# 64-wide products of a blockwise triangular inverse in 32-wide halves, with other owners for its block copies and a few scales and sums moved

## The chip, the cores and the metric

The kernel runs on one core of a Trainium2 chip. A core has five engines that run their own instruction streams and meet through semaphores: PE (TensorE, matrix products and transposes into PSUM), DVE (VectorE), ACT (ScalarE), POOL (GpSimd) and SP (SyncE, which here only issues DMA). The metric is the device time of one launch in microseconds (us); lower is better.

## The reference

The input x has 4 sequences of 1024 tokens with 128 channels. Everything is f32. Cut to what matters:

```python
def _layernorm(x, axis=-1, eps=1e-05):
    ...
    return (x - m) / jnp.sqrt(v + eps)

def delta(x, gates_w, gates_b, lr_w, lr_b, out_w, out_b):
    qkv = x @ gates_w + gates_b
    q, k, v = jnp.split(qkv, 3, axis=-1)
    lr = x @ lr_w + lr_b
    k = k / jnp.linalg.norm(k, axis=-1, keepdims=True)
    K = jnp.tril(jnp.einsum('ntc,nsc->nts', k, k), k=-1)
    A = K + jnp.eye(T, dtype=x.dtype)
    u = jax.scipy.linalg.solve_triangular(A, v, lower=True)
    score = jnp.einsum('nsk,ntk->nst', q, k)
    y = jnp.einsum('nst,ntv->nsv', score, lr * u)
    return y @ out_w + out_b
...
h = _layernorm(x)
h = h + delta(layernorm(h, dn_g, dn_b), ...)
h = h + mlp(layernorm(h, mn_g, mn_b), w1, b1, w2, b2)
x = x + h
h = _layernorm(x)
# top-1 of 8 experts by h @ gate_w.T, each a 128x128 matrix
x = x + h + expert_out_of_the_chosen_expert(h)
```

## The kernel before

Tokens are cut into T = 8 tiles of 128 tokens. A tile holds the same 128 tokens of all NS = 4 sequences, so most steps of a tile are four products of 128x128, or one instruction over 512 columns. `LOW` means sequences 0 and 1, `HIGH` 2 and 3. The tiles form two groups g of TG = 4.

**Front.** For each tile DVE takes the statistics (`stats`), ACT a square root (`root`), DVE the reciprocal (`scales`), and POOL, ACT and DVE share the normalised rows `xh`. PE turns them (`xT_`), ACT copies them out (`xnT_`), PE projects them to k (`kT_`), ACT copies that, and PE multiplies k by its own transpose (`gram`) into a 128x128 matrix per sequence, which ACT copies to `gg_all`. `k_` turns k back.

**Inverse of the unit triangular matrix.** Its 128 rows are four blocks b of 32. The diagonal 32x32 blocks of a whole group (16 matrices, four blocks each, 128 partitions) are gathered into `gd`: 26 small DMAs on SP in all, ten of them for group 0, and three copies on ACT and three on DVE. `prepare(0)` on DVE waits for all of these. DVE then inverts all blocks of the group at once: `prepare`, the 31 steps of `eliminate`, and two transposes into `d_all` (the inverse, `plain_`) and `dT_all` (its transpose, `turned`). The blocks must then stand at their places in `tt_all` (the 128x128 transposed inverse of a tile) and `da_all` (inverses as a left operand). For the group's first tile DVE (`place`) and ACT (`plain_place`, `turned_place`) copy them, for the other three tiles six DMAs on SP do.

**Joining.** For each tile, blocks are joined to 64 and then to 128: `ya` (eight products of 32x32), `za` (twelve), `y64_` (four of 64x64), `t12` (four of 64x64), each followed by a copy out of PSUM under the same name on ACT, and for `yb`, `zb` and `t12` on ACT in group 0 and on DVE in group 1.

**Recurrence.** The state S runs over the tiles: `ks` (k times state, PE), `rv_` (DVE, the right-hand side), `w_` (inverse times it, PE; ACT copies), `lrw` (ACT, times the learning rate), `s_` (PE, adds to the state; ACT copies it out as `sm`). The joins of tile t+1 stand between these. While group 1 is being eliminated on DVE, tiles 1 to 3 of the recurrence run, and `rv_all(1)`, `rv_all(2)` and `rv_all(3)` stand between the steps of `eliminate(1)` and behind it.

**The rest.** After the last tile the state is folded with the weights (`mm`, `mw`, `gn`), and each tile goes through h (normalised x, `h_` on DVE for HIGH, POOL for LOW) plus delta (`h2_`), statistics, scale and bias (`hscale`, `hbias`), MLP, again statistics, and the experts, with `copy_predicated` on DVE. POOL makes the sums `xb2_` (x plus a bias) and `xb_` (plus h) into `x_all`.

All orders are written out by hand; every engine executes its own list in that order. Nothing is scheduled by a planner.

## Time and profile before

| | us |
|---|---|
| median of three runs | 202.74 (202.15 to 202.99) |
| the profiled execution, its own time | 201.71 |
| its span | 199.8 |
| PE busy | 179.8 (90%) |
| DVE busy | 166.3 (83%) |
| ACT busy | 114.4 (57%) |
| POOL busy | 63.7 (32%) |

The span is what the profiler sees between the first and the last instruction; the execution's own time lies 1.9 us above it. The parts follow one another in time: the front to about 23 us for group 0 (35 us for group 1), values and preparations to 51, the recurrence to 98, the fold and the first tile of the rest to 112, the steady loop of the rest to 186, its tail to the end. Times of a row are counted from the span's start.

### The profile page before, as it was taken

The numbers are of one execution on the slowest core, as the hardware profiler recorded it, in microseconds if no ns is written. First come the engines' busy times: TensorE is split into PE (matmuls) and PEld (weight loads), VectorE is DVE, ScalarE is ACT, GpSimd is POOL, SyncE is SP. The second block draws the span as 40 slices with busy tenths as digits, with TensorE's granted clock in tenths as the row PEclk, the third lists the DMA queues.
The fourth block names the chain that finished last, engine by engine and source line by source line (L and its number), as shares of the span: only waits on it lengthen the run. The fifth ranks groups of instructions, "written<-read, shape, count | busy, mean of one in ns | idle before, by whom it ended". The sixth has DMA issues, their size and how long they took to land.

```text
span 199.8 us, 4189 instructions
## 1 busy us (share of the span) xinstructions
PE 179.8 (90%) x1299; PEld 130.7 (65%) x1299; DVE 166.3 (83%) x750; ACT 114.4 (57%) x318; POOL 63.7 (32%) x79
## 2 busy tenths in 40 slices
PE   0498799999999899999998999999999999999980
PEld 0355676887988677877864776766667675657540
DVE  7898899999899945494686688898989899878885
ACT  2567786588795785457327763645456363752420
POOL 8256980000000069980022220070605233202030
PEclk9999999999999999999999999999999999999997
DMA  4982011103000030000000000010101001011011
GB/s 115 302 211 29 10 16 20 21 5 59 3 2 3 0 61 1 3 3 3 0 2 0 3 0 0 0 54 3 53 0 36 18 5 53 0 53 53 0 54 53
DMA packets 20265, 6.53 MB, mean 33 GB/s; under 512 B 9995, under 2 KB 20244, under 8 KB 20244
## 3 DMA queue, kind: packets, MB, share of 16 engines
q1 hardware_dynamic: 19668, 6.21, 13.1%
q8 instruction: 10, 0.16, 0.4%
q10 hardware_dynamic: 576, 0.07, 0.2%
q14 instruction: 11, 0.09, 0.1%
HBM read 3.15 MB, written 2.10 MB: 26 GB/s over the span
## 4 chain that ended last, share of the span: by engine, by line
PE 62%; DVE 17%; ACT 5%; issue 3%; DVEq 0%; ACTq 0%
PE ps L1390 25%; PE ps L1104 10%; PE ps L1298 5%; PE ps L1099 5%; PE ps L1369 4%; DVE kT_all L1022 3%; DVE xi L836 3%; DVE prod L829 3%; PE ps L1133 2%; PE ps L1288 2%; DVE rv L885 2%; PE ps L1226 2%; PE ps L1282 2%; PE ps L1213 2%; PE ps L1116 1%
## 5 line engine op out<-in xcount | busy, mean ns | idle before, releaser
L1390 PE MATMUL ps<-ewC,kT_all 128*128 128x256 f32 (+2 forms) x192 | 62.0, 455 | 0.7 <-DVE kT_all L1022 0.7
L1022 DVE COPY_PREDICATED kT_all<-mask,ps 128x256 f32<-128x256 int32 x112 | 49.1, 439 | 2.6 <-DVE mask L1008 0.3
L1390 PEld LDWEIGHTS ps<-ewC,kT_all 128*128 128x128 f32 x192 | 33.9, 190 | 16.6 <-issue 6.0
L359 POOL TENSOR_TENSOR x_all<-x_all,kT_all 128x512 f32<-128x512 f32 (+1 forms) x8 | 9.6, 1204 | 54.6 <-ACT kT_all L679 54.6
L836 DVE TENSOR_TENSOR xi<-xi,prod 128x60 f32<-128x60 f32 (+13 forms) x116 | 19.6, 207 | 0.3
L829 DVE TENSOR_TENSOR prod<-lts,xi 128x60 f32<-128x60 f32 (+13 forms) x116 | 19.3, 204 | 0.3
L353 POOL TENSOR_TENSOR x_all<-x_all,h_all 128x512 f32<-128x512 f32 (+1 forms) x9 | 10.3, 1150 | 24.6 <-DVE h_all L954 19.9
L1298 PE MATMUL ps<-ww,k_all 128*128 128x256 f32 (+1 forms) x72 | 17.1, 365 | 0.4 <-DVE ww L939 0.4
L322 POOL TENSOR_SCALAR h_all<-x_all,mv,rr 128x128 f32<-128x128 f32 x18 | 14.6, 822 | 7.5 <-DVE rr L751 7.5
L649 ACT ACTIVATE k_all<-h_all,nb,rr 128x128 f32<-128x128 f32 x32 | 13.4, 483 | 1.9 <-DVE nb L975 1.5
L336 POOL TENSOR_SCALAR bob<-bob 128x128 f32<-128x128 f32 x1 | 0.5, 528 | 42.5 <-DVE da_all L859 42.5
L340 POOL TENSOR_SCALAR h_all<-x_all,mv,rr 128x128 f32<-128x128 f32 x16 | 12.5, 795 | 0.0
L1099 PE MATMUL ps<-ident,h_all 128*128 128x128 f32 x32 | 5.8, 312 | 7.3 <-ACT h_all L390 7.2
L1298 PEld LDWEIGHTS ps<-ww,k_all 128*128 128x128 f32 x72 | 11.1, 189 | 2.0 <-DVE ww L939 0.5
L1099 PEld LDWEIGHTS ps<-ident,h_all 128*128 128x128 f32 x32 | 4.4, 160 | 12.1 <-issue 12.0
L638 ACT ACTIVATE sd<-mv,epsc 128x4 f32<-128x4 f32 (+1 forms) x9 | 2.6, 294 | 15.0 <-DVE mv L966 15.0
L655 ACT ACTIVATE k_all<-ps,cols 128x512 f32<-128x512 f32 (+1 forms) x9 | 6.6, 730 | 8.1 <-PE ps L1099 8.1
L1104 PE MATMUL ps<-kT_all 128*128 128x128 f32 x64 | 9.5, 292 | 1.9 <-ACT kT_all L399 1.8
L679 ACT ACTIVATE kT_all<-kT_all,rr 128x128 f32<-128x128 f32 x30 | 9.5, 388 | 2.3 <-DVE kT_all L1022 2.3
L559 ACT ACTIVATE ww<-ww,v_all 128x128 f32<-128x128 f32 x28 | 10.7, 407 | 0.1
L666 ACT COPY kT_all<-ps 128x512 f32<-128x512 f32 (+1 forms) x9 | 4.8, 535 | 10.0 <-PE ps L1099 10.0
L1104 PEld LDWEIGHTS ps<-kT_all 128*128 128x128 f32 x64 | 8.0, 196 | 3.7 <-ACT kT_all L399 3.4
(156 smaller groups left out, 389.9 us busy)
## 6 DMA issues: line engine op xcount, KB each, us to landing
x_all<-in_L_attn_x_dram SPq DMA_DIRECT2D x7, 256.0 KB, 5.4
out_dram<-x_all SPq DMA_DIRECT2D x7, 256.0 KB, 2.3
ew<-in_L_ffn_expert_w_dram SPq DMA_DIRECT2D x1, 512.0 KB
gd<-gg_all SPq DMA_DIRECT2D x26, 16.0 KB, 1.8
tt_all<-dT_all SPq DMA_DIRECT2D x8, 48.0 KB, 2.1
x_all<-in_L_attn_x_dram SPq DMA_DIRECT2D x2, 128.0 KB, 2.8
out_dram<-x_all SPq DMA_DIRECT2D x2, 128.0 KB, 1.8
da_all<-d_all SPq DMA_DIRECT2D x4, 48.0 KB, 2.1
```

The lines of the kernel that those rows point to most:

```text
L322: nc.gpsimd.tensor_scalar(xh[:, t, n], x_all[:, t, n], mv[:, 0, t, n, 0:1], rr[:, t, 1, n:n + 1], ALU.subtract, ALU.mult).then_inc(xh_pool, 1)
L340: last = nc.gpsimd.tensor_scalar(h_all[:, t, n], x_all[:, t, n], mv[:, 0, t, n, 0:1], rr[:, t, 0, n:n + 1], ALU.subtract, ALU.mult)
L353: nc.gpsimd.tensor_tensor(x_all[:, t, span(of)], x_all[:, t, span(of)], h_all[:, t, span(of)], ALU.add).then_inc(xb_ready, len(of))
L559: nc.scalar.mul(ww[t % 2][:, n, C:2 * C], ww[t % 2][:, n, 0:C], v_all[:, t, n, C:VW]).then_inc(lrw_ready, 1)
L649: nc.scalar.activation(tn[t % 2][:, n], h_all[:, t, n], ACT.Identity, bias=nb2[:, t, n:n + 1], scale=rr2[:, 0, t, n:n + 1]).then_inc(tn_re ...
L829: nc.vector.tensor_tensor(mul[half], lts[:, j, lo:hi].unsqueeze(2).broadcast_to([P, hi - lo, w]), xi[g][:, j, 0:w].unsqueeze(1).broadcast_ ...
L836: nc.vector.tensor_tensor(xi[g][:, lo:hi, 0:w], xi[g][:, lo:hi, 0:w], mul[half], ALU.subtract).then_inc(elim, 1)
L1022: nc.vector.copy_predicated(sel[t % 2][:, n], mask[t % 2][:, n, E - 1 - e].unsqueeze(2).broadcast_to([P, 2, F]), expert(e)).then_inc(picke ...
L1099: last = nc.tensor.transpose(tiles(bank)[:, n], src(n), ident[:])
L1104: last = nc.tensor.matmul(tiles(bank)[:, n], lhsT(n), rhs(n), start=True, stop=True)
L1298: last = nc.tensor.matmul(both(n)[:, of], k_all[:, t, n], ww[t % 2][:, n, of], start=t == 0 and n % 2 == 0 and of.start == 0, stop=True, s ...
L1390: last = nc.tensor.matmul(dst, x1T[t % 2][:, 2 * pair + n], ewC[:, of], start=True, stop=True)
```

## The change

- `y64_` and `t12` on PE multiply with 32 moving columns instead of 64: each 64x64 product becomes two of 64x32. The halves of `y64_` go to PSUM partitions 0 to 63 and 64 to 127, so that ACT copies [128 x 128] instead of [64 x 256]; the halves of `t12` read partitions 0 to 63 and 64 to 127, and write to banks 6 and 7. For this `da_all` has all 128 partitions, with its blocks there twice: `za` has one more product per sequence and its copy one more instruction on ACT, and two more DMAs per group. `ya` now also waits for the copy of the tile before's `t12`.
- Placing for the first tile of a group: DVE's `place` is gone; ACT places three blocks (`plain_place`, `odd_place`), SP's DMAs the rest, of all four tiles. SP issues eight DMAs a group instead of six, in another order, the ones for `t12` ahead of those for the next tile's `ya`.
- Front: for the first three tiles `gram` and its copy stand one tile later; `k_` stands one tile earlier from there on.
- Scales: `root` and `scales` only treat the scale of the doubly normalised rows; that of h is made once for all tiles, by one add and one reciprocal on DVE and one square root on ACT, while tile 4 is joined. `nb` is only made where ACT reads it. POOL's `h_` therefore waits for `first_rr`.
- DVE: 12 and 11 elimination steps instead of 10 and 12 between the `rv_all` of group 1, and `rv_all(3)` ahead of the two transposes. At tile 4, `ya`, `za`, `y64_` and `t12` stand later on PE, and DVE's `rv` on both sides of `zb`. `h_` of the last two tiles stands behind the last `ww`.
- POOL's first `xb_` wait for the first tile's `hbias` (`hnb_done`).

Front, PE, from the first projection on (`xnT_all,gall` is `kT_`, `ident,h_all` is `xT_`, `kT_all` alone is `gram`, `ident,kT_all` is `k_`). Before:

```order
L1116 MATMUL ps<-xnT_all,gall 128x512
L1099 MATMUL ps<-ident,h_all 128x128 x4
L1104 MATMUL ps<-kT_all 128x128 x4
L1116 MATMUL ps<-xnT_all,gall 128x512
L1099 MATMUL ps<-ident,h_all 128x128 x4
L1104 MATMUL ps<-kT_all 128x128 x4
```

Now:

```order
L1144 MATMUL ps<-xnT_all,gall 128x512
L1127 MATMUL ps<-ident,h_all 128x128 x4
L1144 MATMUL ps<-xnT_all,gall 128x512
L1127 MATMUL ps<-ident,h_all 128x128 x4
L1132 MATMUL ps<-kT_all 128x128 x4
L1144 MATMUL ps<-xnT_all,gall 128x512
L1127 MATMUL ps<-ident,h_all 128x128 x4
L1132 MATMUL ps<-kT_all 128x128 x8
```

The first `gram` stands behind the second tile's `kT_` and the third's `xT_`; the second and third follow each other.

DVE, from the end of the second elimination to the first reciprocal for POOL (`rv<-v_all,nk,ps` is `rv_`; `d_all`, `dT_all` the two transposes; `yT` is `yb`; a `tt_all<-ps` of 32 is `zb`, of 64 `t12`). Before:

```order
L844 STREAM_TRANSPOSE d_all<-xi 128x32x16
L849 STREAM_TRANSPOSE dT_all<-d_all 128x512
L885 SCALAR_TENSOR_TENSOR rv<-v_all,nk,ps 128x128 x4
L858 COPY tt_all<-dT_all 32x4x32 x2
L859 COPY da_all<-d_all 32x4x32
L867 COPY yT<-ps 32x128
L863 STREAM_TRANSPOSE nk<-nkl 128x32
L872 TENSOR_SCALAR tt_all<-ps 32x4x32
L885 SCALAR_TENSOR_TENSOR rv<-v_all,nk,ps 128x128 x4
L878 TENSOR_SCALAR tt_all<-ps 64x4x64
```

Now:

```order
L906 SCALAR_TENSOR_TENSOR rv<-v_all,nk,ps 128x128 x4
L874 STREAM_TRANSPOSE d_all<-xi 128x32x16
L879 STREAM_TRANSPOSE dT_all<-d_all 128x512
L884 STREAM_TRANSPOSE nk<-nkl 128x32
L888 COPY yT<-ps 32x128
L939 TENSOR_SCALAR ab<-mv 128x8x4
L906 SCALAR_TENSOR_TENSOR rv<-v_all,nk,ps 128x128 x2
L893 TENSOR_SCALAR tt_all<-ps 32x4x32
L906 SCALAR_TENSOR_TENSOR rv<-v_all,nk,ps 128x128 x2
L899 TENSOR_SCALAR tt_all<-ps 64x2x4x32
L948 RECIPROCAL rr<-sd 128x8x4
```

The `rv` of tile 3 is ahead of the transposes, the placing copies are gone, and the reciprocal that POOL waits for stands behind `t12` of tile 4.

PE at the same place (`rv,tt_all` is `w_`, `ww,k_all` is `s_`, `sm,kT_all` is `ks`, `tt_all,gg_all` of 32 is `ya`; `yT` and `da_all` rows are `za`), before (the `za` rows that repeat are left out):

```order
L1288 MATMUL ps<-rv,tt_all 128x128 x4
L1181 MATMUL ps<-tt_all,gg_all 32x32 x8
L1298 MATMUL ps<-ww,k_all 128x256 x2
L1195 MATMUL ps<-yT,d_all 32x32
...
L1298 MATMUL ps<-ww,k_all 128x256 x2
L1213 MATMUL ps<-tt_all,gg_all 64x64 x4
L1282 MATMUL ps<-sm,kT_all 128x128 x4
L1226 MATMUL ps<-y,da_all 64x64 x4
L1181 MATMUL ps<-tt_all,gg_all 32x32 x8
L1288 MATMUL ps<-rv,tt_all 128x128 x4
```

Now:

```order
L1322 MATMUL ps<-rv,tt_all 128x128 x4
L1332 MATMUL ps<-ww,k_all 128x256 x4
L1210 MATMUL ps<-tt_all,gg_all 32x32 x8
L1316 MATMUL ps<-sm,kT_all 128x128 x2
L1224 MATMUL ps<-yT,d_all 32x32
...
L1316 MATMUL ps<-sm,kT_all 128x128 x2
L1242 MATMUL ps<-tt_all,gg_all 64x32 x8
L1254 MATMUL ps<-y,da_all 64x32 x8
L1210 MATMUL ps<-tt_all,gg_all 32x32 x8
L1322 MATMUL ps<-rv,tt_all 128x128 x4
```

All four joins of tile 4 now stand behind the state update of tile 3.

The diff, cut to its core:

```diff
@@ the blocks of one tile on SP @@
             sp.wait_ge(tt_clear, 2)
+            sp.wait_ge(da_clear, 1)
             for g in range(NG):
+                def turned(b, lo):
+                    r = slice(Q * b, Q * b + Q)
+                    return by_block(tt_all, g, r, b, lo), dT_all[g][r, lo * NS:GN]
+
+                def plain(b, at, lo):
+                    r, place = slice(Q * b, Q * b + Q), slice(Q * at, Q * at + Q)
+                    return by_block(da_all, g, place, b, lo), d_all[g][r, lo * NS:GN]
+
+                sp.wait_ge(d_done, g + 1)
+                dst, src = plain(1, 1, 0)
+                sp.dma_start(dst, src).then_inc(rest_sent[g], 16)
                 sp.wait_ge(dT_done, g + 1)
...
-                for (dst, src), sent in ((turned(1), odd_sent), (turned(3), odd_sent), (plain(0), even_sent),
-                                         (turned(2), even_sent), (plain(1), rest_sent), (turned(0), rest_sent)):
+                for (dst, src), sent in ((turned(2, 0), two_sent), (turned(0, 0), rest_sent), (plain(0, 2, 0), rest_sent),
+                                         (plain(1, 3, 0), rest_sent), (turned(1, 1), odd_sent), (turned(3, 1), odd_sent),
+                                         (plain(0, 0, 1), zero_sent)):
                     sp.dma_start(dst, src).then_inc(sent[g], 16)
@@ POOL @@
-            pool.wait_ge(tt_dve, NG)
+            pool.wait_ge(dT_done, NG)
...
             pool.wait_ge(xT_mm, T)
+            pool.wait_ge(first_rr, 1)
...
+            pool.wait_ge(hnb_done, 2)
             xb_(0, LOW)
+            pool.wait_ge(hnb_done, NS)
             xb_(0, HIGH)
@@ ACT: the front, the copies of za and y64, tile 4 @@
-            for t in range(T):
+            for t in range(TG):
                 if t == TG - 2:
                     root(4)
                 kT_(t)
                 if t == TG - 1:
                     root(5)
-                if t + 1 < T:
-                    xnT_(t + 1)
+                xnT_(t + 1)
                 if t == 0:
                     root(3)
                 if t + 2 < TG:
                     xh_(t + 2)
-
-                if t >= TG:
-                    k_(t - TG)
+                if 0 < t < TG - 1:
+                    gg_(t - 1)
+                if t == TG - 2:
+                    gd_(t)
+                    gg_(t)
+            gd_(TG - 1)
+            k_(0)
...
-                nc.scalar.mul(da_all[Q:2 * Q, t, :, 0:Q],
-                              ps[Q:2 * Q, 6, 2 * NS * Q:3 * NS * Q].rearrange("p (n c) -> p n c", n=NS), -1.0).then_inc(za_ready, 1)
+                for b in (1, 3):
+                    r = slice(Q * b, Q * b + Q)
+                    last = nc.scalar.mul(da_all[r, t, :, 0:Q],
+                                         ps[r, 6, 2 * NS * Q:3 * NS * Q].rearrange("p (n c) -> p n c", n=NS), -1.0)
+                last.then_inc(za_ready, 1)
...
                 if t == TG - 1:
+
+                    s_(t, 0)
+                    odd_place(1)
                     s_(t, 1)
+                    plain_place(1)
+                    ya(t + 1)
+                    za(t + 1)
                     y64_(t + 1)
+                    act.wait_ge(first_ab, 1)
+                    nc.scalar.activation(sd[:, :, 0], ab[:, :, 0], ACT.Sqrt).then_inc(first_sd, 1)
@@ DVE @@
-            place(0)
 
             prepare(1)
-            eliminate(1, 0, 10)
+            eliminate(1, 0, 12)
             dve.wait_ge(nk_done, 1)
             dve.wait_ge(v_ready, T)
             rv_all(1)
-            eliminate(1, 10, 22)
+            eliminate(1, 12, 23)
             rv_all(2)
-            eliminate(1, 22, Q - 1)
+            eliminate(1, 23, Q - 1)
+            rv_all(3)
             plain_(1)
             turned(1)
-            rv_all(3)
-            place(1)
...
+            h_(T - 2)
+            h_(T - 1)
             dve.wait_ge(mw_mm, 2)
@@ PE: the joins @@
                 for n in range(NS):
-                    last = nc.tensor.matmul(ps[0:2 * Q, 7, 2 * n * Q:2 * (n + 1) * Q], gg_all[2 * Q:4 * Q, t, n, 0:2 * Q],
-                                            tt_all[2 * Q:4 * Q, t, n, 2 * Q:4 * Q], start=True, stop=True)
+                    for h in range(2):
+                        last = nc.tensor.matmul(ps[2 * Q * h:2 * Q * h + 2 * Q, 7, n * Q:n * Q + Q], gg_all[2 * Q:4 * Q, t, n, 0:2 * Q],
+                                                tt_all[2 * Q:4 * Q, t, n, (2 + h) * Q:(3 + h) * Q], start=True, stop=True)
                 last.then_inc(y64_mm, 1)
...
                 for n in range(NS):
-                    last = nc.tensor.matmul(ps[0:2 * Q, 7, 2 * (NS + n) * Q:2 * (NS + n + 1) * Q], da_all[:, t, n],
-                                            y64[t % 2][:, n], start=True, stop=True)
+                    for h in range(2):
+                        r = slice(2 * Q * h, 2 * Q * h + 2 * Q)
+                        last = nc.tensor.matmul(ps[0:2 * Q, 6 + h, (3 * NS + n) * Q:(3 * NS + n + 1) * Q], da_all[r, t, n],
+                                                y64[t % 2][r, n], start=True, stop=True)
```

## Rows read from the trace of the kernel before

**Rows 1.** The page: the span, and the shares of the chain that ended last.
```profile
span 199.8 us, 4189 instructions
PE 62%; DVE 17%; ACT 5%; issue 3%; DVEq 0%; ACTq 0%
```

**Rows 2.** That chain in order: start us, length us, what.
```profile
77.33 1.13 PE ps L1288 x8
```

**Rows 3.** Timeline, front: start us, us, engine, line, out<-in, count, idle before.
```profile
12.49 3.12 POOL L322 TENSOR_SCALAR h_all<-x_all,mv,rr 128x128 f32<-128x128 f32 x4 [2.14 <-DVE rr L751]
...
13.54 0.58 ACT L415 COPY gg_all<-ps 128x512 f32<-128x512 f32 x1 [0.20 <-PE ps L1104]
...
23.35 1.96 DVE L802 STREAM_TRANSPOSE lt<-gd 128x1024 f32<-128x1024 f32 x1
```

**Rows 4.** SP's DMAs issued between 17 and 19.5 us; landings of that line.
```profile
17.04 2.53 SPq L270 DMA_DIRECT2D gd<-gg_all  x4
...
DMA to landing us min/median/max: 1.8/1.8/2.9
```

**Rows 5.** Timeline of DVE, from the first inverse's transpose to the second group.
```profile
44.11 0.71 DVE L849 STREAM_TRANSPOSE dT_all<-d_all 128x512 f32<-128x512 f32 x1
...
45.64 1.95 DVE L802 STREAM_TRANSPOSE lt<-gd 128x1024 f32<-128x1024 f32 x1
```

**Rows 6.** Timeline during the second elimination: DVE, and PE's weights of one ks.
```profile
55.17 1.12 DVE L885 SCALAR_TENSOR_TENSOR rv<-v_all,nk,ps 128x128 f32<-128x128 f32 x4 [0.97 <-PE ps L1282]
...
62.65 1.11 DVE L885 SCALAR_TENSOR_TENSOR rv<-v_all,nk,ps 128x128 f32<-128x128 f32 x4
...
68.05 0.97 PEld L1282 LDWEIGHTS ps<-sm,kT_all 128*128 128x128 f32 x8
...
69.65 1.08 DVE L885 SCALAR_TENSOR_TENSOR rv<-v_all,nk,ps 128x128 f32<-128x128 f32 x4
```

**Rows 7.** Timeline of PE and ACT, one tile of group 1: joins and copies.
```profile
79.83 0.68 PE L1213 MATMUL ps<-tt_all,gg_all 64*64 64x64 f32 x8
80.44 1.13 PE L1298 MATMUL ps<-ww,k_all 128*128 128x256 f32 x4
...
83.19 0.44 PE L1181 MATMUL ps<-tt_all,gg_all 32*32 32x32 f32 x16
...
79.97 0.27 ACT L496 ACTIVATE da_all<-ps 32x128 f32<-32x128 f32 x1
```

**Rows 8.** Weight loads, each: ns min/median/max, first and last start us, form.
```profile
L1213 PEld LDWEIGHTS ps<-tt_all,gg_all x64: 129/135/136, 47.9 to 92.7; 64*64 64x64 f32 x64
...
L1159 PEld LDWEIGHTS ps<-gwT,cent x2: 186/188/189, 42.2 to 42.3; 128*128 128x128 f32 x2
```

**Rows 9.** Timeline of PE at 42 us: loads of 128 columns for 8 moving ones.
```profile
42.19 0.30 PEld L1159 LDWEIGHTS ps<-gwT,cent 128*128 128x128 f32 x2 [0.44 <-ACT ewT L465]
```

**Rows 10.** Timeline of DVE, then of POOL: the scales and sums of h.
```profile
79.19 1.33 DVE L890 TENSOR_SCALAR h_all<-x_all,mv,rr 128x128 f32<-128x128 f32 x4
...
85.44 3.39 DVE L890 TENSOR_SCALAR h_all<-x_all,mv,rr 128x128 f32<-128x128 f32 x4
...
72.05 12.50 POOL L340 TENSOR_SCALAR h_all<-x_all,mv,rr 128x128 f32<-128x128 f32 x16
84.52 2.48 POOL L347 TENSOR_TENSOR x_all<-x_all,b2s 128x512 f32<-128x512 f32 x2
```

**Rows 11.** Timeline of DVE at the last tile of the recurrence.
```profile
94.72 0.42 DVE L878 TENSOR_SCALAR tt_all<-ps 64x256 f32<-64x256 f32 x1 [1.91 <-PE ps L1226]
...
96.18 1.11 DVE L890 TENSOR_SCALAR h_all<-x_all,mv,rr 128x128 f32<-128x128 f32 x4
```

**Rows 12.** Timeline of DVE, biases of the first and second tile, and POOL beside.
```profile
105.31 1.23 DVE L975 SCALAR_TENSOR_TENSOR nb<-mv,rr 128x2 f32<-128x2 f32 x1
...
109.96 0.16 DVE L975 SCALAR_TENSOR_TENSOR nb<-mv,rr 128x4 f32<-128x4 f32 x1
...
105.26 1.27 POOL L353 TENSOR_TENSOR x_all<-x_all,h_all 128x512 f32<-128x512 f32 x1 [1.45 <-DVE h_all L954]
```

182 lines of the change are left out of this document (93 added, 89 removed).

## The prediction

> **What bounds the kernel now.** I read the page first: PE holds 62% and DVE 17% of the chain that ended last [rows 1]. That is an average; read in order of time, the chain changes engines four times, and the edits lie only in the first 110 us. Up to 23.35 us the front ends with the gathering of `gd`, on which DVE's first elimination waits [rows 3]. From there to about 70 us DVE works almost without a gap; its one gap inside the second elimination is 0.97 us ahead of `rv_all(1)` [rows 6]. From the `w_` of tile 4, at 77.33 us [rows 2], to 98 us PE is full. From 98 to 110 us the first tile's chain of small steps decides, and behind it comes the loop that the change leaves alone. So I follow four times: the start of the first elimination, the three `rv_all`, the `w_` of tiles 4 and 7, and the second bias.
>
> **Front.** Three things make the old path shorter: each stage of the statistics and each `nb` loses a short instruction, and `gram` no longer holds up PE. By my count of the chain DVE could transpose `gd` at about 22.0. But the first copy to `gg_all` started at 13.54 and now stands behind the turned rows of tile 2. POOL makes two of these from 12.49, 0.78 us each, so until 14.05 [rows 3], now some 0.5 sooner for the instructions left out (taken, not measured; with 0 it all comes 0.5 later); then `xT_` (about 0.7), `gram` (about 1.1), and ACT's copies ahead put `gg_all` at 15.5 to 16.1. It was done at 14.1, so the first gathering DMA goes out 2.0 us later. SP issues four in 2.53 us, 0.63 to 0.65 each, and each lands 1.8 us after its issue [rows 4]. Group 0 needs ten: 16.1 + 9 x 0.65 + 1.8 = 23.75. In the kernel before the first went out at about 14.3, but SP idled ahead of tiles 1 and 2, and the tenth landed at about 22.5, hidden behind DVE. Now the DMAs are the last to end: **+0.4 us** instead of -1.3. The bounds: -0.3 if `gg_all` starts 0.7 sooner, +1.3 if the second `kT_` still runs at the slow pace of the first (one us longer), because PE has less to do ahead of it.
>
> **The first inverse to `rv_all(1)`.** `place` goes from DVE: the turned inverse is done at 44.82 and the next group's transpose begins at 45.64 [rows 5], so 0.8 us of DVE are free. The joins of tiles 0 and 1, however, hang on PE and ACT: `rv_all(1)` came at 55.17, 10.35 us behind the turned inverse. ACT's three placing copies cost what DVE's did; the fifth DMA of the eight, the last that `t12` needs, is issued 0.1 + 3 x 0.65 us behind the turned inverse and lands 2.1 later, at +4.2, against +4.9 when `t12` ran. `za` costs ACT one copy of 0.27 us more per tile [rows 7], the copy of `y64_` perhaps 0.1 less. I keep 10.35: `rv_all(1)` at 55.17 + 0.4 = 55.6. DVE's elimination stood idle for 0.97 us there; now it does two steps more, of (62.65 - 56.25) / 12 = 0.53 us each [rows 6], and is ready at 54.9. So it is 1.07 - 0.4 = 0.65 us ahead in work. **`rv_all(2)`**: 55.6 + 1.05 + 11 x 0.53 = 62.5, with one step more done. **`rv_all(3)`** no longer waits for the transposes but for `ks` of tile 3. Its weights loaded at 68.05, 5.4 us behind `rv_all(2)` [rows 6]; that gives 68.35, where it was 69.65: **-1.3 us**. DVE waits there (eight steps end at 67.3), and the inverse ends at 68.35 + 1.1 + 1.85 = 71.3, not 69.7.
>
> **Tile 4.** Here the gain is used up. Before, `ya` and `za` of tile 4 ran between the products of tile 3. Now `w_` of tile 3 starts at 68.7, its `s_` ends 3.5 later at 72.2 (1.3 until ACT has copied and scaled the first two, then two halves of 1.13 at best [rows 7]), ACT copies the state and places a block (0.3 to 0.4 each), and only then, at 72.9, comes `ya`. From there in one chain: `ya` 0.44, copy 0.28, `za` 0.4, copy 0.28, `y64_` 0.68, copy 0.27, `t12` 0.68 and its copy 0.42 [rows 7, 11], with some 0.07 between each two: 76.9. `ya` of tile 5 now waits for that copy and stands ahead of `w_`: 77.3. It was 77.33 [rows 2]. Net **0**, with bounds of -0.6 and +0.6.
>
> **Halves of the joins.** The trace has no 64x32 product. A 64-wide product takes 0.68 us for eight instructions [rows 7]; a product of 8 moving columns with 128 weight columns has its two loads 0.11 us apart [rows 9], so below the load's own time fewer moving columns buy nothing. A load takes 53 ns more at 128 columns than at 64 [rows 8], so 64 columns need about 55 ns, near what an instruction takes today. The 32-wide `ya` does two products to different parts of the array in 33 ns (16 in 0.44 [rows 7]), so halves do run side by side. Eight pairs of 55 ns: **0**. Lower bound 33 ns a pair, -0.2 us a product; upper bound all sixteen in a row, +0.45.
>
> **POOL's scales later.** POOL started them at 72.05, and they took 12.50, then its sums came; now it starts at 77.4, so the sums lie from 89.9 to 95. DVE's four `h_` take 1.33 beside POOL's scales and 3.39 beside its sums [rows 10]. The slow ones move from tile 6's joins, where PE had other work, to those of tile 7, which have no `ya` behind them: `h_` from 91.7 to 95.1 lets the copy of `t12`, at 94.72 [rows 11], start at 95.15: **+0.45 us**. Then the last `h_` no longer stand between `rv` and `ww`: 1.11 us [rows 11], of which 0.2 turns into waiting for `w_`: **-0.9**. Their new place, ahead of a copy that waits over a us, costs nothing as long as POOL's sums are over by 97.
>
> The rows show no blocking beside POOL's scales. The Trainium skill (SBUF — State Buffer, Who interferes with whom) says that a DVE scale in its two-port mode and any GpSimd instruction exclude each other. By that rule `h_` of two more tiles would be slow and the new wait of `ya` for `t12`'s copy would turn this into about 0.5 us; the sum goes by the rows.
>
> **The first bias.** `hbias` of HIGH took 1.23 us beside POOL's `xb_`, 0.16 alone [rows 12]. POOL now waits for it: -1.07, and -0.3 for the LOW one, of which ACT's order lets about 1.0 through: **-1.0 us**. POOL's sums end near 107.5, ahead of the first use.
>
> **The sum.** 0 (tile 4) + 0.45 - 0.9 - 1.0 = -1.45 us. The profiled execution took 201.71 with a span of 199.8, 1.0 under the median of 202.74; the shift goes on the median: 202.74 - 1.45 = **201.3 us**.
>
> **Rivals.** *The halves queue up.* If two halves with the same rows (`y64_`) or columns (`t12`) don't overlap, each product costs +0.45. For one of the two kinds: four tiles of group 1 on PE's path, 1.8, and about three places in the chain of tiles 0 to 3, 1.2: 201.3 + 3.0 = 204.3, slower than before. It decides from about 0.25 us a product. Against it: `za` already has two products with the same rows at different columns. 10%. The Trainium skill (TensorE: Matmul & The Clock Gate, Part 3) says a weight load overlaps a running product only where the row group differs, which would be this for `y64_`.
> *The halves gain.* At 33 ns a pair, -0.2 a product: eight in group 1, 1.6, and 0.5 ahead: 199.2. For it: pairs of `ya`; against it: the load. 20%.
> *The DMAs are hidden anyway.* If `gg_all` comes earlier or SP issues faster, the first elimination starts at 22.0: -1.8, so 199.5. 8%.
> *PE stays slow for another projection*: +0.9, 202.2. 12%.
>
> **Chances.** The forecast has 50%, with a range of its own from 200.4 to 202.2. The range reaches to the gaining halves and past the slow projection: 199.1 to 202.8. A measurement of this kernel tells 0.5%, 1.0 us, from no change. Faster by more: 0.38 of the forecast's 0.50, 0.20 and 0.08 of two rivals, less a little for the long list of steps: 0.64. Within: 0.26. Slower: 0.10.
>
> **What would show it.** Ten `gd` DMAs without a gap on SP, and the transpose of `gd` right behind the last landing, at 23.6 to 24.0; DVE idle for 0.7 ahead of `rv_all(1)` and 1.0 ahead of `rv_all(3)`; `w_` of tile 4 at 77 to 77.6; eight-pair joins of 0.6 to 0.7 us; `h_` of 3.4 us near 92; both first biases at 0.16. It is wrong if `gd` is transposed before 23, or if a join's product takes under 0.5 or over 0.9.

## The result and the profile after

| | before | after |
|---|---|---|
| median of four runs, us | 202.44 (201.68 to 202.99) | 206.75 (205.16 to 207.46) |
| the profiled execution, its own time | 201.71 | 207.46 |
| its span | 199.8 | 205.4 |
| mean granted clock of PE | 0.993 | 0.977 |

The change makes the kernel slower: the ratio after to before is 1.020, with a 95% interval of 1.015 to 1.025. Forecast were 201.3 us, so the sign is wrong too. In all four executions of the changed kernel the mean granted clock was 0.976 or 0.977. (Ratios, here and below, leave disturbed executions out, so that one can lie below the ratio of the medians.)

The page of the changed kernel, the lines that answer to [rows 1]:

```profile
span 205.4 us, 4576 instructions
PE 62%; DVE 18%; DMA 6%; SPq 6%; ACT 4%; issue 3%; DVEq 0%; ACTq 0%
```

DMA and SP's queue now hold 12% of the chain that ended last; in [rows 1] neither appears. Where that is, the timeline tells. First the front (columns as in [rows 3]):

```profile
12.25 3.24 POOL L331 TENSOR_SCALAR h_all<-x_all,mv,rr 128x128 f32<-128x128 f32 x4 [1.76 <-DVE rr L782]
...
12.94 2.08 PE L1144 MATMUL ps<-xnT_all,gall 128*128 128x512 f32 x2 [0.78 <-ACT xnT_all L408]
...
17.62 0.58 ACT L430 COPY gg_all<-ps 128x512 f32<-128x512 f32 x1 [0.64 <-PE ps L1132]
...
18.23 12.03 SPq L275 DMA_DIRECT2D gd<-gg_all  x14
...
26.04 1.98 DVE L832 STREAM_TRANSPOSE lt<-gd 128x1024 f32<-128x1024 f32 x1 [1.49 <-DMA gd<-gg_all]
```

The first copy to `gg_all` stood at 13.54 us and is now at 17.62; `gd` is transposed at 26.04 where it was 23.35, behind a wait of 1.49 us for its transfers. Then the DVE in the recurrence, which answers to [rows 5, 6]:

```profile
46.85 0.71 DVE L879 STREAM_TRANSPOSE dT_all<-d_all 128x512 f32<-128x512 f32 x1
...
58.18 1.12 DVE L906 SCALAR_TENSOR_TENSOR rv<-v_all,nk,ps 128x128 f32<-128x128 f32 x4 [1.12 <-PE ps L1316]
...
65.18 1.12 DVE L906 SCALAR_TENSOR_TENSOR rv<-v_all,nk,ps 128x128 f32<-128x128 f32 x4
...
71.72 1.12 DVE L906 SCALAR_TENSOR_TENSOR rv<-v_all,nk,ps 128x128 f32<-128x128 f32 x4 [1.85 <-PE ps L1316]
```

Tile 4, the timeline of PE and DVE:

```profile
76.48 0.44 PE L1210 MATMUL ps<-tt_all,gg_all 32*32 32x32 f32 x16 [0.92 <-ACT da_all L502]
...
79.54 0.91 PE L1254 MATMUL ps<-y,da_all 64*64 64x32 f32 x16 [0.36 <-ACT y L538]
...
80.49 0.42 DVE L899 TENSOR_SCALAR tt_all<-ps 64x256 f32<-64x256 f32 x1 [1.39 <-PE ps L1254]
...
81.77 0.64 PE L1210 MATMUL ps<-tt_all,gg_all 32*32 32x32 f32 x16 [1.31 <-DMA tt_all<-dT_all]
...
82.33 2.08 PE L1322 MATMUL ps<-rv,tt_all 128*128 128x128 f32 x8
```

`ya` of tile 4 waits for a block that ACT places, `t12` for ACT's copy, `ya` of tile 5 for a transfer, and only then comes `w_` of tile 4, at 82.33 where [rows 2] had 77.33. It takes 2.08 us where it took 1.13. The table by stretches says why (us from and to; busy us of PE with its instructions, PE's weight loads, DVE, ACT, POOL; then the granted clock of PE, DMA share, GB/s):

```profile
74.00:76.00 2.00, 1.57 (x8) 0.95 (x6) 0.70 (x2) 1.89 (x7) 0.53 (x1) 1.00 0.25 38
76.00:78.00 2.00, 1.51 (x53) 1.31 (x54) 0.94 (x4) 0.66 (x3) 0.00 (x0) 1.00 0.63 97
78.00:80.00 2.00, 1.64 (x32) 1.40 (x34) 1.03 (x4) 1.20 (x5) 0.00 (x0) 0.94 0.55 88
80.00:82.00 2.00, 0.69 (x19) 0.55 (x16) 0.68 (x2) 0.00 (x0) 0.65 (x1) 0.50 0.16 22
...
84.00:86.00 2.00, 2.00 (x37) 1.53 (x37) 0.96 (x4) 1.98 (x9) 2.00 (x4) 0.50 0.01 4
86.00:88.00 2.00, 2.00 (x22) 1.39 (x21) 0.87 (x3) 0.69 (x3) 2.00 (x4) 0.85 0.00 0
```

From 74 to 80 us PE is busy for 4.72 of 6 us, in short pieces. Just ahead of 80 us the granted clock falls from 1.00 to 0.50, that is from 2.4 to 1.2 GHz, and it comes back at about 86.6, though PE has been busy without a gap since 81.8. The transfers of the second group of inverses, issued between 70 and 82 us (KB each, median us from issue to landing), and the one for which `ya` of tile 5 waited, from the chain (start, length):

```profile
da_all<-d_all SPq DMA_DIRECT2D x3, 64.0 KB, 2.2
tt_all<-dT_all SPq DMA_DIRECT2D x2, 64.0 KB, 2.2
tt_all<-dT_all SPq DMA_DIRECT2D x2, 48.0 KB, 2.9
da_all<-d_all SPq DMA_DIRECT2D x1, 48.0 KB, 3.3
```

```profile
77.96 3.76 DMA tt_all<-dT_all
```

The sixth and seventh of the eight bring blocks 1 and 3, which `ya` of tile 5 needs. The last of them was issued 4.06 us behind the start of `turned`, for whose result the queue waits (`dT_all`, 73.90), and took 3.76. In group 0 of the same execution the seventh took 2.1.

The products themselves, one tile of group 1, against [rows 7, 8]:

```profile
86.79 0.65 PE L1242 MATMUL ps<-tt_all,gg_all 64*64 64x32 f32 x16
...
88.44 0.66 PE L1254 MATMUL ps<-y,da_all 64*64 64x32 f32 x16
```

```profile
L1242 PEld LDWEIGHTS ps<-tt_all,gg_all x128: 129/135/135, 50.5 to 99.6; 64*64 64x64 f32 x128
```

The profile counts two instructions to an f32 product: the sixteen of eight halves take what the eight of four whole products took, 0.65 against 0.68 us. And the end, against [rows 10 to 12]:

```profile
93.77 4.94 POOL L357 TENSOR_TENSOR x_all<-x_all,b2s 128x512 f32<-128x512 f32 x4
...
98.59 1.11 DVE L911 TENSOR_SCALAR h_all<-x_all,mv,rr 128x128 f32<-128x128 f32 x4
...
109.90 0.16 DVE L1003 SCALAR_TENSOR_TENSOR nb<-mv,rr 128x2 f32<-128x2 f32 x1
...
111.73 0.16 DVE L1003 SCALAR_TENSOR_TENSOR nb<-mv,rr 128x2 f32<-128x2 f32 x1 [0.29 <-DVE rr L999]
```

Both first biases take 0.16 us where the second of them took 1.23.

Laid end to end, the two profiled executions differ so (start to start, us; the first and last pieces reach to the ends of the span):

| stretch | before | after | difference |
|---|---|---|---|
| start to the transpose of `gd` | 23.35 | 26.04 | +2.69 |
| to `rv_all(1)` | 31.82 | 32.14 | +0.32 |
| `rv_all(1)` to `rv_all(3)` | 14.48 | 13.54 | -0.94 |
| `rv_all(3)` to `w_` of tile 4 | 7.68 | 10.61 | +2.93 |
| `w_` of tile 4 to tile 5 | 6.23 | 8.15 | +1.92 |
| `w_` of tile 5 to tile 7 | 12.05 | 11.98 | -0.07 |
| `w_` of tile 7 to the third bias (109.96, 115.43) | 14.35 | 12.97 | -1.38 |
| to the end | 89.84 | 89.97 | +0.13 |
| span | 199.8 | 205.4 | +5.6 |

Three places lose: the front, the way into tile 4, and the products behind it. One gains as foreseen. The experiments take them apart. Their times are medians, and each stands beside runs of the kernel before on the same chip, whose medians were 201.98 to 202.26 us.

### The profile page after: what moved, and what is told of

It reads as the page before. It is cut to its first block, busy times and chain, and to the rows that moved or that the text cites. A ratio compares the mean times of both kernels' runs of the same rounds, so it can differ in the third digit from the quotient of the medians.

```text
span 205.4 us, 4576 instructions
## 1 busy us (share of the span) xinstructions
PE 183.7 (89%) x1491; PEld 134.5 (65%) x1491; DVE 161.0 (78%) x732; ACT 116.3 (57%) x327; POOL 63.6 (31%) x79
## 2 busy tenths in 40 slices
DMA packets 23146, 6.91 MB, mean 34 GB/s; under 512 B 12875, under 2 KB 23124, under 8 KB 23124
## 4 chain that ended last, share of the span: by engine, by line
PE 62%; DVE 18%; DMA 6%; SPq 6%; ACT 4%; issue 3%; DVEq 0%; ACTq 0%
PE ps L1428 25%; PE ps L1132 8%; PE ps L1332 6%; PE ps L1127 4%; PE ps L1407 4%; DVE xi L866 4%; DVE prod L859 4%; PE ps L1322 4%; DVE kT_all L1050 3%; PE ps L1316 3%; SPq L275 3%; DMA x_all<-in_L_attn_x_dram 2%; SPq L297 2%; PE ps L1254 2%; PE ps L1144 2%
## 5 line engine op out<-in xcount | busy, mean ns | idle before, releaser
L1332 PE MATMUL ps<-ww,k_all 128*128 128x256 f32 (+1 forms) x72 | 17.7, 377 | 0.1
L1127 PEld LDWEIGHTS ps<-ident,h_all 128*128 128x128 f32 x32 | 4.9, 171 | 12.2 <-issue 12.2
L1144 PE MATMUL ps<-xnT_all,gall 128*128 128x512 f32 x16 | 10.8, 768 | 1.0 <-ACT xnT_all L408 1.0
L906 DVE SCALAR_TENSOR_TENSOR rv<-v_all,nk,ps 128x128 f32<-128x128 f32 x28 | 8.0, 344 | 3.0 <-PE ps L1316 3.0
```

The source lines that it names most:

```text
L1127: last = nc.tensor.transpose(tiles(bank)[:, n], src(n), ident[:])
L1144: nc.tensor.matmul(ps[:, 1, :], gall[:, C:2 * C], rows(xnT_all[:, t]), start=True, stop=True).then_inc(kT_mm, 1)
L1332: last = nc.tensor.matmul(both(n)[:, of], k_all[:, t, n], ww[t % 2][:, n, of], start=t == 0 and n % 2 == 0 and of.start == 0, stop=True, s ...
```

## The experiments

### The front

**Undo the front.** The changed kernel with k k^T in the place it had before:

```diff
-            for t in range(TG):
-                kT_(t)
-                xT_(t + 1)
-                if 0 < t < TG - 1:
-                    gram(t - 1)
+            for t in range(T):
+                kT_(t)
+                if t + 1 < T:
+                    xT_(t + 1)
+                if t >= TG:
+                    k_(t - TG)
+                gram(t)
```

> The changed kernel, with the front's order of the kernel before (each gram behind its own kT_, k_ where it stood). Theory A (the later gram left PE with too little work, its second and third projections ran at half pace, 2.08 and 1.50 us instead of 1.02, and the first copy to gg_all and with it ten gathering DMAs came 4 us late): projections at 1.02 again, the transpose of gd at 22 to 22.5 us instead of 26.04, everything behind it shifts by 3.5 to 4; time about 203. Rival B (the fewer scales or SP's queue delay the gathering whatever PE does): the transpose stays near 25 to 26 us and the time near 206.5.

Measured: 208.9 us, ratio 1.032 (1.028 to 1.037). The front does what was expected: the first copy to `gg_all` at 13.56, `gd` transposed at 22.68 (3.4 us sooner), `rv_all(3)` at 68.85 (2.9 sooner). Yet the kernel is 2 us slower than the changed one. The stretches show where it went; the granted clock is the third number from the end:

```profile
78.00:80.00 2.00, 1.58 (x20) 1.51 (x21) 0.33 (x2) 0.43 (x2) 1.78 (x3) 0.50 0.00 0
...
88.00:90.00 2.00, 2.00 (x24) 1.77 (x23) 1.46 (x5) 0.00 (x0) 2.00 (x4) 0.50 0.00 0
90.00:92.00 2.00, 2.00 (x47) 1.81 (x44) 0.32 (x2) 1.11 (x5) 2.00 (x3) 0.69 0.00 0
```

PE ran at 1.2 GHz for some 13.5 us instead of 6.8, and `w_` of tile 5 came 11.16 us behind that of tile 4 instead of 8.15. The time of about 203 us that was expected is missed by 6, though its mechanism in the front holds. So the front's loss is real, and the larger matter lies at tile 4, where a gain ahead of it can turn into a loss.

**The front's new order alone**, in the kernel before (the same lines, the other way round).

> The kernel before with the changed kernel's front order alone. Theory A: second projection 2.0 us long, gd transposed at 25.5 to 26.5 us instead of 23.35, time 2.5 to 3 us above the kernel before. Rival B (the order itself is harmless and only the mix of the edits costs): within 0.5 us of the kernel before.

Measured: 203.33 us, ratio 1.006 (1.003 to 1.009), +1.3 us. `gd` was transposed at 24.14, behind 1.47 us of waiting for its transfers, though the second projection took only 1.12 us in this execution. The 2.5 to 3 us of theory A are not reached. The wait for the transfers is there without a slow projection, and the slow projection comes on top: across the profiled executions with the new order and nothing added in the front, `gd` stood at 24.14 and 24.29 where the second projection took 1.12 and 1.13, and at 25.90 to 26.11 where it took 2.08.

The slow pace doesn't need the new order. In three profiled executions with the old one the second projection took 1.31 (tile 4's order alone), 1.48 (both changes at the end) and 1.68 us (the change without its reorderings, sums later) instead of 1.02. The times show it too, as far as they go: the ten executions here lie in two clusters, 202.5 to 203.0 and 203.6 to 204.6, and the profiled one, at full pace, is the lowest (202.53). Nine of the ten with tile 4's order undone lie at 201.6 to 201.8 (two) and 203.3 to 203.9 (seven), with the profiled one, at slow pace, among the upper. So medians of few executions can differ by which pace they caught. That the pace makes the clusters isn't shown, since only one execution of each kernel was profiled. It isn't the granted clock as the profile has it, which reads 1.00 from 6 to 21 us in all of these.

**Fill PE's wait in the front.** Four unused products behind the turned rows of tile 1:

```diff
                 xT_(t + 1)
+                if t == 0:
+                    for _i in range(4):
+                        nc.tensor.matmul(ps[:, 6, 0:C], ident[:], ident[:], start=True, stop=True)
```

> The changed kernel with four extra 128x128 products of the identity on PE behind the second xT_, into a bank that nobody reads before it is written anew; gram stays late. Theory A (it is PE's missing work): the second projection takes 1.0 us, or the third does, gg_all is first copied 1 to 2 us sooner (16 to 17 us), gd is transposed at 24 to 25, time 1 to 2 us below the changed kernel. Rival C (it is only that gram stands later in order, the pace is fixed by time since the start): projections stay slow, gd at 26 us, time unchanged within 0.5.

Measured: 207.69 us over four executions that lie at 205.02, 205.14, 210.23 and 216.55; ratio 1.014 (1.010 to 1.018), against 1.020 (1.015 to 1.025) of the changed kernel, whose lowest execution took 205.16. In the profiled execution the second projection took 1.81 us and `gd` stood at 25.11, but that was the one of 216.55 us, too far off the others to rest anything on. The intervals overlap as well. Whether keeping PE busy there gives anything is not shown.

### Tile 4

**Blocks 1 and 3 sent first.** In group 1, SP issues the two transfers for which `ya` of tile 5 waited ahead of three that `t12` of tile 4 needs:

```diff
-                for (dst, src), sent in ((turned(2, 0), two_sent), (turned(0, 0), rest_sent), (plain(0, 2, 0), rest_sent),
-                                         (plain(1, 3, 0), rest_sent), (turned(1, 1), odd_sent), (turned(3, 1), odd_sent),
+                for (dst, src), sent in ((turned(2, 0), two_sent), (turned(1, 1), odd_sent), (turned(3, 1), odd_sent),
+                                         (turned(0, 0), rest_sent), (plain(0, 2, 0), rest_sent),
+                                         (plain(1, 3, 0), rest_sent),
```

> The changed kernel with group 1's two odd-block DMAs issued second and third of eight, not sixth and seventh. Theory D (in group 1 ya of tile 5 waits until 81.72 us for the odd block's DMA, PE goes idle and then runs at half clock until 86): ya of tile 5 starts at 80.95, w_ of tile 4 at 81.4 instead of 82.33, and if the wait is what drops the clock, also w_ at 1.1 us again, so 1 to 3 us less. Rival E (the clock falls because of the earlier gaps between 73 and 81 us, behind s_ of tile 3 and between the joins): 0.8 us less at most, w_ of tile 4 still near 2 us long; t12 may wait for the DMAs that now come later.

Measured: 214.93 us as the median of 212.34, 212.63, 217.22 and 217.3; even the lowest, which is the profiled one, is 4.9 us over the slowest of the changed kernel. The wait went where the second theory feared it. The transfers that moved back are those for which `t12` of tile 4 itself waits:

```profile
81.36 1.07 PE L1257 MATMUL ps<-y,da_all 64*64 64x32 f32 x16 [2.32 <-DMA da_all<-d_all]
...
83.02 0.64 PE L1213 MATMUL ps<-tt_all,gg_all 32*32 32x32 f32 x16 [0.60 <-DVE tt_all L902]
```

`w_` of tile 4 came at 83.59, and the granted clock stayed at 0.50 from 79 to 96 us. Two transfers must land for `ya` of tile 5, four for `t12` of tile 4, and in either order of the queue one of the two joins waits. Other orders were not run.

**Tile 4's order undone**, the rest of the change kept:

```diff
-            rv_all(3)
             plain_(1)
             turned(1)
-            norms(1)
+            rv_all(3)
             yb(TG)
+            norms(1)
+            zb(TG)
...
+            odd_place(1)
+            plain_place(1)
             for t in range(TG - 1, T - 1):
...
-                if t + 1 != TG:
+                if t + 1 == TG:
+                    ya(t + 1)
+                else:
                     za(t + 1)
                 for n in LOW:
                     s_(t, n)
```

> The changed kernel with the order of tile 4's joins as before on all three engines: the DVE makes d_all and dT_all of the second group ahead of rv_all(3), ACT places the blocks ahead of w_(3), and PE runs ya(4) ahead of s_(3), za(4) in its middle and y64_(4) behind it, so that only t12(4) is left between ks(4) and w_(4). Theory 'clock at tile 4': in the changed kernel PE stood idle 4.3 of the 10 us from 72 to 82 us of its span, its granted clock fell to 0.50 and stayed there to 86 us, which cost 2.9 us up to w_(4) and 1.9 us from w_(4) to w_(5). With the old order the granted clock stays 1.00, w_(4) stands about 7.7 us behind rv_all(3) and w_(5) 6.3 us behind w_(4), and the median is near 202.2 us. Theory 'front alone' (the late k k^T is what costs, and tile 4 only passes it on): the time stays within 1 us of 206.7.

Measured: 203.51 us, ratio 1.006 (1.003 to 1.009). So 3.2 us of the loss are gone. `w_(3)` to `w_(4)` took 7.31 us (10.14 in the changed kernel), `w_(4)` to `w_(5)` 6.22 (8.15), and the clock stayed at 1.00 there. Forecast were 202.2; 0.9 us of the difference comes between `w_(6)` and `w_(7)`, see below.

**Only PE's gaps filled.** The direct question to the clock: nothing undone, but 13 unused products on PE where it waited.

```diff
+            def spare(count):
+                for i in range(count):
+                    nc.tensor.matmul(ps[:, i % 2, 2 * C:3 * C], ident[:], ident[:], start=True, stop=True)
...
                 if t == TG:
                     y64_(t)
+                    spare(2)
                     t12(t)
+                    spare(6)
...
                 if t + 1 == TG:
+                    spare(5)
                     ya(t + 1)
```

> The changed kernel with 13 added 128x128 products on PE that nobody reads: 5 ahead of ya(4), 2 between y64_(4) and t12(4), 6 behind t12(4), where PE waited. They take about 0.18 us each at full clock and nothing else is changed. Theory 'clock at tile 4': with the gaps filled the granted clock stays 1.00 or falls for a shorter time than the 80 to 86 us of the changed kernel; w_(4) takes 1.1 us in place of 2.08, w_(4) to w_(5) 6.3 us in place of 8.15, and the median is near 204. Theory 'waits alone' (the waits for ACT and the DMA are the loss, the clock is beside the point): the products only get in the way, and the median is 206.7 to 207.5.

Measured: 204.86 us, ratio 1.015 (1.010 to 1.020), 1.9 us under the changed kernel. The two intervals overlap, and the profiled execution had its second projection at full pace (`gd` at 24.29), which the changed kernel's had not. What carries the reading is the clock: its mean was 0.995 to 0.997 in all four executions, against 0.976 and 0.977 in the four of the changed kernel, and the profile has it at 1.00 from 70 to 100 us:

```profile
78.00:80.00 2.00, 2.00 (x30) 1.89 (x28) 0.68 (x2) 0.00 (x0) 0.37 (x1) 1.00 0.18 26
80.00:82.00 2.00, 2.00 (x59) 1.72 (x57) 0.29 (x1) 1.16 (x6) 2.00 (x4) 1.00 0.00 0
```

`w_(4)` to `w_(5)` takes 6.22 us, not 8.15: that is 1.93 us, as much as the medians differ, and it is the price of the clock. `w_(3)` to `w_(4)` stays at 10.18 us. There the unused products stand on PE's path themselves: in the chain they hold 1.11 us ahead of `ya`, 0.64 ahead of `t12` and 1.53 behind it, so this kernel can't tell what the waits that they cover would cost without them.

**And `ya` of tile 5 behind `w_` of tile 4**, on top of the filled gaps:

```diff
-                if t + 1 < T and t + 1 != TG:
+                if t + 1 < T and t + 1 != TG and t != TG:
                     ya(t + 1)
                 for n in range(NS):
                     w_(t, n)
+                if t == TG:
+                    ya(t + 1)
```

> The changed kernel with the 13 added products at tile 4, and ya(5) moved behind w_(4) on PE and on ACT, so that w_(4) no longer stands behind the wait for the transfers of blocks 1 and 3 (in the changed kernel t12(4)'s last copy ended at 80.91 us and w_(4) began at 82.33, behind ya(5), which waited 1.31 us for them). Theory 'the transfer is a wait of its own': w_(4) begins some 1.3 us sooner after w_(3), 8.9 us in place of 10.2, w_(4) to w_(5) stays near 6.2 to 6.6, and the median is 203.6 to 204.0, against 204.9 with the products alone. Rival 'what is late is the whole row of joins': w_(4) is sooner, but ya(5), za(5), y64(5) and t12(5) then stand late ahead of w_(5), and the gain is given back there: 204.9.

Measured: 205.77 us (1.017, 1.012 to 1.022). `w_(3)` to `w_(4)` fell by 0.47 to 9.71 us, and `w_(4)` to `w_(5)` grew by 0.97 to 7.19. The sum of both stretches is 16.90 us against 16.40, so nothing was gained, as the rival says. But the experiment can't decide between the two: the last unused products stand ahead of `w_(4)` and keep PE busy to 82.1 us, while the seventh transfer lands at 81.7 (issued at 78.0, 3.7 us), so `w_` could come forward by little more than `ya` itself. Whether the transfer is a wait of its own stays open; `ya` behind `w_` without the filling was not run. The slow projection is back in this profile (`gd` at 26.09), and three of its four times lie at 205.7 to 206.1, the fourth at 204.2.

**The front undone and the gaps filled**, edits as above:

> The changed kernel with k k^T in the front as before and the 13 added products at tile 4. With the front undone alone the kernel took 208.9 us, since the granted clock fell to 0.50 at 78 us and stayed there to about 91. Theory 'the front's 2.2 us are there, and the longer fall of the clock hid them': with the clock kept up by the products, the median is 204.9 less 2.2, so 202.7, and the granted clock is 1.00 from 70 to 96 us. Rival 'the old front makes tile 4 wait longer by itself': w_(3) to w_(4) is over 11 us even at full clock, and the median is 204 or more.

Measured: 203.66 us (1.007, 1.004 to 1.011): 1.2 us under the filled kernel with the late k k^T, and 5.2 under the same kernel without the filling (208.9). `w_(4)` to `w_(5)` was 6.22 again. These intervals lie far apart (1.004 to 1.011 against 1.028 to 1.037), so this pair is the firm proof that filling PE's gaps gives back what the clock cost. The front's gain was there all along, hidden behind the longer fall of the clock. The 2.2 us that were expected are not reached. With the second projection at full pace in both profiles, the front's order costs 0.9 us at `rv_all(3)` (69.92 against 69.03), as in the kernel before (70.55 against 69.65); what the medians show beyond that, 1.2 and 1.3 us, may be the slow pace of some executions.

**Both orders undone**, edits as above:

> The changed kernel with both orders as before: k k^T in the first four tiles, and tile 4's joins. What is left of the change is the halves of 64, the blocks placed by ACT and by 8 DMAs in place of 6, the first scales' part on POOL, and the two changes at the end (h_ of the last two tiles behind the last ww, POOL's sums behind the first tile's scales). If the front costs 2.7 us and tile 4's clock 4.7 us, the median is near 200.5 us, 1.5 us under the kernel before, and the end of the chain after w_(7) is 1.5 us shorter than in the kernel before. If the halves or the extra DMAs cost something of their own (the DMAs landed up to 3.8 us after their issue in the changed kernel), it is 202 us or more.

Measured: 201.35 us, ratio 0.996 (0.994 to 0.999): 2.2 us under the kernel with tile 4's order undone alone. Here the second projection took 1.02 us. The change without its two reorderings is thus a small gain.

**Tile 4's order alone**, in the kernel before, with joins of 64 columns and six transfers:

```diff
+            rv_all(3)
             plain_(1)
             turned(1)
-            rv_all(3)
             place(1)
...
-                if t + 1 == TG:
-                    ya(t + 1)
-                else:
+                if t + 1 != TG:
                     za(t + 1)
```

> The kernel before with tile 4's order of the changed kernel on all three engines and nothing else of the change: rv_all(3) ahead of the second group's last transposes, the placing copies among tile 3's state copies, ya(4) behind s_(3), za(4) between the halves of ks(4), y64_(4) and t12(4) behind them. The joins are the 64-wide ones and the transfers are the six of before. Theory 'the order alone does it': PE waits in the row of joins as in the changed kernel, w_(3) to w_(4) is 9.5 to 10.5 us in place of 7.3, the granted clock falls to 0.50 near tile 4 in the profiled run, and the median is 204.5 to 207 us. Rival 'it needed the eight transfers': with six, ya(5) finds its blocks, and the clock stays up; w_(3) to w_(4) is 9 us and the median is 203 to 203.8.

Measured: 202.83 us, ratio 1.003 (1.002 to 1.005). Neither theory as written: it was better than the second, and far better than the first. PE hardly waits, and the clock stays up:

```profile
76.00:78.00 2.00, 1.31 (x28) 1.09 (x27) 0.71 (x2) 0.62 (x2) 2.00 (x4) 1.00 0.31 45
```

```profile
77.80 1.13 PE L1292 MATMUL ps<-rv,tt_all 128*128 128x128 f32 x8 [0.23 <-DVE tt_all L879]
...
85.91 4.82 DVE L891 TENSOR_SCALAR h_all<-x_all,mv,rr 128x128 f32<-128x128 f32 x4
...
86.42 2.48 POOL L347 TENSOR_TENSOR x_all<-x_all,b2s 128x512 f32<-128x512 f32 x2
```

`w_(3)` to `w_(4)` is 7.74 us, `w_(2)` to `w_(4)` even 0.5 shorter than before. The kernel before has the two transfers for `ya` of tile 5 first in its queue, and places tile 4's own blocks by copies, so no join of tile 4 waits for SP. **The order alone does no harm; it needs other parts of the change.** Laid beside the changed kernel, two pieces between `w_(3)` and `w_(4)` differ: `ya` of tile 4 starts 3.31 us behind `w_(3)`, not 4.29, since DVE and not ACT places the blocks that it needs, and `ya` of tile 5 starts 0.60 us behind `t12`, not 2.23, since it waits neither for the copy of `t12` nor for the seventh transfer. Which of these three (ACT's placing, the new wait for `t12`'s copy, the queue of eight) does the harm was not taken apart. With the old order the queue and the placing did none: there `w_(3)` to `w_(4)` took 7.31 us. What this kernel loses, it loses between `w_(5)` and `w_(6)` (7.45 us instead of 6.25), to an `h_` of 4.82 us beside POOL's sums.

### The end, and POOL

**Both changes at the end alone**, in the kernel before:

```diff
-                h_(2 * (t - TG))
-                h_(2 * (t - TG) + 1)
                 if t + 1 < T:
+                    h_(2 * (t - TG))
+                    h_(2 * (t - TG) + 1)
                     t12(t + 1)
...
                                         ALU.mult).then_inc(lrw_last, 1)
+            h_(T - 2)
+            h_(T - 1)
...
+            pool.wait_ge(hnb_done, 2)
             xb_(0, LOW)
+            pool.wait_ge(hnb_done, NS)
             xb_(0, HIGH)
```

> The kernel before with only the two changes at the end: h_ of the last two tiles behind the ww of tile 7 on the DVE, and POOL's sums of the first tile behind its scales (waits on hnb_done). Theory: h_ behind ww gives 0.75 to 0.9 us and the first bias on the DVE, no longer beside POOL's sums, 0.8 to 1.0, so 200.3 to 200.6 us. Rival: POOL's later sums make x1_ of the first tiles wait, and the gain of the second is given back: 201.2 us. Rival: neither is on the chain of the kernel before, 202.0.

Measured: 200.84 us, ratio 0.995 (0.993 to 0.997). The stretch from `w_(7)` to the third bias is 12.97 us, as in the changed kernel.

**`h_` late alone** (the first two pieces of that diff):

> The kernel before with h_ of the last two tiles behind the last ww of tile 7, and nothing else. Both changes at the end together gave 1.16 us. If each gives what was forecast in proportion (0.9 and 1.0), this one gives about 0.55: 201.4 us. If h_ is all of it: 200.8. If POOL's waits are all of it: 202.0.

Measured: 202.29 us (1.002, 1.000 to 1.004). The stretch is 14.02 us, 0.33 shorter, and the median shows nothing of it.

**POOL's waits alone** (the last piece):

> The kernel before with POOL's sums of the first tile behind its scales, and nothing else. h_ late alone measured 202.3 us, with a profiled stretch from w_(7) to the second bias of 14.02 us against 14.35; both together 200.8 and 12.97. Theory 'POOL's waits are nearly all of it': the stretch is 13.2 to 13.4 us, and the median is 200.8 to 201.1 us. Rival 'each needs the other': above 201.5.

Measured: 201.05 us (0.995, 0.993 to 0.997), the stretch 13.41 us: 0.94 of the 1.38. Nearly all that can be measured is POOL's. The late `h_` could give no more, because in the kernel before PE waited only 0.35 us for the `ww` behind it:

```profile
97.60 0.75 PE L1298 MATMUL ps<-ww,k_all 128*128 128x128 f32 x4 [0.35 <-DVE ww L939]
```

**The late scales with both changes at the end.** To the kernel before are added: scales of k alone in the front, no bias for tiles 4 to 7, and the first normalization's sum, root and reciprocal in one piece at tile 4, on which POOL waits.

```diff
-                nc.vector.reciprocal(rr[:, lo:hi], sd[:, lo:hi]).then_inc(rr_done, 1)
+                nc.vector.reciprocal(rr[:, lo:hi, 1], sd[:, lo:hi, 1]).then_inc(rr_done, 1)
...
             pool.wait_ge(xT_mm, T)
+            pool.wait_ge(first_rr, 1)
```

> The kernel before with the two changes at the end and with the first normalization's scales made late in one piece (the scales of k alone in the front, no bias for tiles 4 to 7), as the changed kernel has them; the joins, placements, DMAs and the front's order are those of before. With both orders undone in the changed kernel, dT_all of the first group stood 0.7 us sooner than in the kernel before. Theory 'the DVE bounds the front': that 0.5 to 0.7 us reaches rv_all(1) here, and the median is 200.1 to 200.3 us. Rival 'PE and ACT bound it too': rv_all(1) stands where it stood, since tiles' joins and copies take the gain; 200.8 us, as the two changes at the end alone. Rival: the late Sqrt, reciprocal and sum stand in the way at tile 4: 201.0 to 201.5.

Measured: 201.08 us (0.995, 0.993 to 0.997), no better than without the late scales. `gd` is transposed at 22.73 and `rv_all(3)` comes at 69.03 (69.65 before), but `w_(6)` to `w_(7)` takes 6.91 us instead of 5.80. The same happens in the kernel with both orders undone:

```profile
88.96 4.95 POOL L357 TENSOR_TENSOR x_all<-x_all,b2s 128x512 f32<-128x512 f32 x4
...
90.74 4.02 DVE L899 TENSOR_SCALAR h_all<-x_all,mv,rr 128x128 f32<-128x128 f32 x4
...
94.79 0.42 DVE L887 TENSOR_SCALAR tt_all<-ps 64x256 f32<-64x256 f32 x1
```

The copy of `t12`, for which `w_(7)` waits, stands behind an `h_` of 4.02 us.

**POOL's first sums behind the last `h_`**, added to that kernel:

```diff
-            for t in range(TG):
+            pool.wait_ge(h_dve, T)
+            for t in range(2):
                 xb2_(t)
...
-                if TG <= t + 2 < T:
+                if t + 2 < T:
                     xb2_(t + 2)
```

> The kernel before with the two changes at the end, the late scales, and POOL's first sums behind the last h_ of the DVE (two tiles there, the others in the loop). With late scales alone the sums lay beside h_(4) and h_(5), which took 4.27 us in place of 1.3, and w_(6) to w_(7) took 6.91 us in place of 5.79; the median was 201.1. Theory: the stretch is 5.8 us again, the gain of the shorter front (0.6 us at rv_all(3)) is left, and the median is 200.0 to 200.3 us. Rival 'the sums now lie beside the first biases or the loop's masks': those are slow instead, and the median is 200.8 to 201.5.

Measured: **199.84 us**, ratio 0.989 (0.987 to 0.990), faster than both kernels.

```profile
91.27 1.12 DVE L895 TENSOR_SCALAR h_all<-x_all,mv,rr 128x128 f32<-128x128 f32 x4
...
97.87 2.49 POOL L349 TENSOR_TENSOR x_all<-x_all,b2s 128x512 f32<-128x512 f32 x2 [8.10 <-DVE h_all L895]
```

`h_` is at 1.12 us, `w_(6)` to `w_(7)` at 5.79, and the stretch behind it at 13.09.

**Only the unread biases dropped**, with both changes at the end:

```diff
-                dve.wait_ge(rr_done, j + 1)
-                for which in range(2):
-                    last = nc.vector.scalar_tensor_tensor(nb[:, lo:hi, which], mv[:, 0, lo:hi, :, 0], -1.0, rr[:, lo:hi, which],
-                                                          ALU.mult, ALU.mult)
-                last.then_inc(nb_done, 1)
+                if lo < TG:
+                    dve.wait_ge(rr_done, j + 1)
+                    nc.vector.scalar_tensor_tensor(nb[:, lo:hi, 1], mv[:, 0, lo:hi, :, 0], -1.0, rr[:, lo:hi, 1],
+                                                   ALU.mult, ALU.mult).then_inc(nb_done, 1)
```

> The kernel before with the two changes at the end, and without the biases that nobody reads: the one of the first normalization for all tiles, and that of k's for tiles 4 to 7, one to two short DVE instructions at each of six stages of the front. POOL's scales stay where they are. Theory 'every short instruction of the DVE in the front counts': dT_all of the first group is 0.3 to 0.5 us sooner, and the median is 200.3 to 200.6 us. Rival 'they are hidden': 200.8.

Measured: 201.25 us (0.995, 0.993 to 0.998), no gain over 200.84 (0.993 to 0.997). DVE waited 0.50 us for `gd`'s transfers at 23.50: what it saves there, it waits there.

**The change without its reorderings, sums later**: the kernel with both orders undone, and POOL's sums moved as above.

> The changed kernel with the front's and tile 4's orders as before and POOL's first sums behind the DVE's last h_. It differs from the kernel before with late scales and later sums (199.84 us) in the halves, the eight transfers, the placing copies on ACT and the small orders of tiles 0 and 1. With both orders undone alone it measured 201.35, with w_(6) to w_(7) 6.67 us. Theory 'halves and transfers cost nothing on the path': w_(6) to w_(7) is 5.8 us, and the median is 199.8 to 200.5 us. Rival 'the halves gain a little, 0.1 us a product in PE's full stretch': 199.3 or less. Rival 'they cost': over 200.8.

Measured: 200.25 us (0.991, 0.988 to 0.994), `w_(6)` to `w_(7)` 5.76 us. Against 199.84 it has the halves, eight transfers and ACT's placing: they cost nothing that can be told, and gain nothing.

**Tile 4's order on the fastest kernel** (joins of 64, six transfers, sums later):

> The kernel before with the two changes at the end, late scales, later sums, and tile 4's order of the changed kernel; joins of 64 columns and six transfers. Alone, that order took w_(2) to w_(4) from 14.2 to 13.7 us in the profiled runs, and then lost 1.2 us to an h_ beside POOL's sums between w_(5) and w_(6). Theory 'the order gives its half us where PE is not left waiting and the sums are elsewhere': 199.2 to 199.6 us, the fastest so far. Rival 'the granted clock falls here too, since everything stands 0.6 us sooner and PE waits at the joins': 201 or more.

Measured: 199.74 us (0.989, 0.987 to 0.992), the same as 199.84. `w_(2)` to `w_(4)` is 13.66 us against 14.18, but `rv_all(1)` and the rest stood 0.36 later in this profile. Neither the half microsecond nor a fall of the clock shows.

## Why the prediction was wrong

**Tile 4** is the step that failed. It forecast `w_(4)` 8.6 us behind `w_(3)` (68.7 to 77.3), and measured 10.14. The row of joins was worked out rightly down to `ya` of tile 4, which came 4.29 us behind `w_(3)` where 4.2 was forecast. Then `t12` took 0.91 instead of 0.68, at the falling clock, and its copy ended 8.72 us behind `w_(3)` instead of 8.2. `ya` of tile 5, which "now waits for that copy and stands ahead of `w_`", was given 0.4 us from there to `w_`; it took 1.42, since it waited for a transfer that the working never looked at: of the eight transfers it had timed only the fifth, for group 0. For group 1 the seventh decides, and it took 3.76 us to land, not 2.1. The bounds of 0.6 to either side held no such case. Undoing tile 4's order gave back 3.2 us of the median.

**PE's clock was no term at all.** The working counted PE's waits as time in which something else runs, to be had back. The price was 1.92 us in the changed kernel, more than any term of the sum. It is shown by the filled gaps: 13 useless products, clock at 1.00, 1.93 us less from `w_(4)` to `w_(5)`; and with the front undone, 5.2 us less by the medians. Together with the wait, tile 4 cost +2.93 and +1.92 us where the working had +1.27 (8.95 behind `rv_all(3)` instead of 7.68) and 0. The Trainium skill (TensorE: Matmul & The Clock Gate, A second HAM failure mode: psum-queue depth-cycling) says that frequent small idle times between groups of products make the clock swing; the trace agrees, since no single wait of PE ahead of the fall was over 0.92 us. That page could have made a rival.

**The front** was the right mechanism, mis-sized. The ten transfers did go out without a gap, and the transpose stood right behind the last landing, as forecast. But it came at 26.04, not at 23.75. The first copy to `gg_all` was put at 15.5 to 16.1 and stood at 17.62, since the second `kT_` took 2.08 us and `xT_` and `gram` behind it were slow as well. That is the rival "PE stays slow for another projection", with 12% and +0.9 us; it cost +1.8 over the same order at full pace (26.04 against 24.14 and 24.29), twice its price, because the turning and the `gram` behind it were slow too and not the projection alone. By medians the order cost 1.3 us in the kernel before, 2.2 with tile 4's order undone and 1.2 with the gaps filled. At full pace the step was right: the first copy stood at 15.77 and 15.87, and the transpose 0.4 to 0.5 behind the forecast 23.75. The step's upper bound of +1.3 was meant for a second projection at slow pace; with it the step came to +2.7.

**From the first inverse to `rv_all(3)`.** "I keep 10.35" measured 10.62. `rv_all(1)` to `rv_all(3)` was to shrink from 14.48 to 12.75 us and shrank to 13.54: DVE did wait there for `ks`, 1.85 us instead of 1.0, but `rv_all(3)` came 6.54 us behind `rv_all(2)`, not 5.85. (The 1.0 is a slip of the working: 62.5 + 1.05 + 8 x 0.53 is 67.8, not 67.3, which leaves 0.5. The forecast doesn't hang on it.) ACT was nearly full there (3.70 of 4 us from 60 to 64), with one more copy per tile for `za`; that this is the reason is not shown.

**Halves**: 0 forecast, 0.65 and 0.66 us against 0.68 measured, and 11.98 us for two tiles against 12.05. The rivals "queue up" and "halves gain" are both out. The Trainium skill (TensorE: Matmul & The Clock Gate, Part 3) has weight loads overlap only where the row group differs; sixteen loads of 135 ns in 0.65 us, eight pairs with the same rows, do not show such a queue.

**POOL's scales later**: +0.45 forecast. In the changed kernel it did not appear, since the delay at tile 4 had put the scales and sums so late (sums from 93.77 to 98.71) that they missed both `h_`. Without that delay it was 0.9 us (both orders undone: 6.67 against 5.76 with the sums later) and 1.1 (6.91 against 5.79): twice the forecast, with the four of an `h_` at 4.02 and 4.27 us instead of 3.4. So there is a hidden third cost. Whoever undoes tile 4's order meets it (6.65 us there); with the gaps filled it is small (5.89).

**The end** was right in sum and partly in parts: -1.38 us in the profile against -0.9 and -1.0 forecast. POOL's waits gave 0.94 and 1.0 in the median, as forecast; the late `h_` gave 0.33, not 0.9. The working took its 1.11 us off the path, less 0.2 for DVE's wait for `w_`; but PE, which sets the path there, had waited only 0.35 us for the `ww` behind it.

Added up over the profiled executions, the forecast is off by 7.05 us (-1.45 against +5.6). Of this 3.4 lie ahead of `rv_all(3)` (2.3 of them in the front), 1.7 between there and `w_(4)`, 1.9 in the clock, and 0.1 behind. Tile 4's wait for the transfer and the clock lie in what the working left out; the front lies in what it counted, at half its price and as a rival. The changed kernel's profile had the slow projection and was the slowest of its four executions, so the front's share is the largest that was seen.

**Left open**: how the wait into tile 4 divides among ACT's placing, `ya`'s new wait for the copy of `t12` and the queue of eight; why the seventh transfer takes 3.1 to 3.8 us in group 1 and 2.1 in group 0; why the clock stays low for 6.8 us in one kernel and 13.5 and 17 in others that differ little, and why the second projection runs slowly in some profiled executions and not in others, with either order.

## What to carry to other kernels

When an edit moves small dependent products out from between large ones, add up PE's waits in their new place, and hold a price for the clock ready: a few gaps of about a microsecond cost 1.9 us here, and as much as 5 in the kernel with the front undone. Test it by filling the gaps with products that nobody reads; if the granted clock stays up and the stretch behind gets shorter, the clock was part of the loss. Such a kernel can't tell what the gaps themselves cost, because the products then stand in them. When transfers replace copies, write down for each consumer which transfer of the queue it needs, and time the last one, not a typical one. And where POOL's two-input sums may slide beside DVE's scales, pin them behind with a wait: that took 1.2 us off (201.08 to 199.84) and gave the fastest kernels here. And before comparing medians of a few executions, look whether they fall into clusters: with tile 4's order undone these lay 1.5 us apart.

## What the runs showed of the hardware

- PE's clock fell from 2.4 to 1.2 GHz behind 4.72 busy of 6 us with no wait over 0.92 us, and stayed low through 4.8 us (changed kernel), 12.8 us (front undone) and 13.0 us (blocks 1 and 3 first) of work without a gap before it rose.
- Four DVE scales of 128x128 took 1.11 us alone, 1.16 to 1.54 beside POOL's scales, and 2.47 to 4.82 where POOL's sums of two inputs lay beside all or some of them. The Trainium skill (SBUF — State Buffer, Who interferes with whom) says that a DVE instruction in a two-port mode and any GpSimd instruction exclude each other; for POOL's sums the traces agree, for its scales they do not. Whether DVE's scales here run in such a mode no trace shows.
- A DVE instruction on 2 elements per partition took 1.23 us beside such a sum, 0.16 us without.
- Transfers from SBUF to SBUF of 48 to 64 KB, eight issued some 0.65 us apart, all landed in 2.1 to 2.3 us in group 0 of the changed kernel. In group 1 the first six did, the seventh took 3.76 and the eighth 3.3; with the gaps filled these two took 3.1 and 2.6. No run shows why.
- Products of 64x32 in pairs cost as much as single ones of 64x64: 0.65 us for sixteen instructions against 0.68 for eight.
